# Two sequences per loop body: query, key and feed-forward projections for both at once, 256 columns wide, as three split float32r products

## What is computed

```python
def _L1_xattn_ref(x, mem_out, ...):
    xn = rms_norm(x, attn_norm_w)
    q, k, v = jnp.split(xn @ to_qkv_w, 3, axis=-1)        # 128 -> 3 * 1024
    q, k, v = (split_heads(q), split_heads(k), split_heads(v))
    q, k = (rope(q), rope(k))
    kf = jnp.concatenate([k_extra, pm, k], axis=2)
    ...
    probs = jax.nn.softmax(scores, axis=-1)
    o = jnp.einsum('bhij,bhjd->bhid', probs, vf)
    x = x + o.transpose(0, 2, 1, 3).reshape(b, n, HEADS * DH) @ to_out_w
    h = rms_norm(x, ff_norm_w) @ ff_w1 + ff_b1             # 128 -> 2 * 341
    a, g = jnp.split(h, 2, axis=-1)
    return x + jax.nn.silu(g) * a @ ff_w2 + ff_b2
```

## Time and profile before

| | |
|---|---|
| median of 3 runs | 1442.05 us (1441.9 to 1442.86) |
| the profiled execution, its own time | 1442.24 us |
| its span, first to last instruction | 1440.5 us |
| mean granted TensorE clock over the span | 0.991 |
| period of a steady turn (one sequence) | 21.21 us |
| DMA queues' share of the 16 engines' time | 27.8% |

### The profile page before, as it was taken

The page is one execution under the profiler, slowest core; times in us unless marked ns, Lnnn a source line. Parts: engine busy times, 40 slices in busy tenths (PEclk is TensorE's granted clock), DMA queues, the critical chain, the costliest instruction groups (busy, mean ns, idle before and its releaser), DMA issues.

```text
span 1440.5 us, 54339 instructions
## 1 busy us (share of the span) xinstructions
PE 1388.4 (96%) x20771; PEld 1225.9 (85%) x20771; DVE 1045.2 (73%) x3025; ACT 790.7 (55%) x1933; POOL 817.6 (57%) x1169
## 2 busy tenths in 40 slices
PE   2699999999999999999999999999999999999997
PEld 1578888988888888898898888889889888888986
DVE  4457777777777777777777777777777777777763
ACT  1245565565556556556556555655655655565553
POOL 1246556556556655655655665565565566566553
PEclk9989999999999999999999999999999999999998
DMA  6323222222322222222232222222222223222210
GB/s 187 113 69 102 101 71 100 101 80 92 103 92 86 100 101 71 100 101 76 96 103 91 87 100 97 75 100 101 74 98 101 87 89 103 93 81 100 101 45 26
DMA packets 106146, 133.13 MB, mean 92 GB/s; under 512 B 16310, under 2 KB 88523, under 8 KB 105995
## 3 DMA queue, kind: packets, MB, share of 16 engines
q1 hardware_dynamic: 106122, 132.81, 27.8%
HBM read 41.04 MB, written 24.61 MB: 46 GB/s over the span
## 4 chain that ended last, share of the span: by engine, by line
PE 94%; DMA 2%; DVE 2%; ACT 1%; SPq 1%; issue 1%; POOL 0%; POOLq 0%; ACTq 0%; DVEq 0%
PE psum L926 16%; PE psum L962 11%; PE psum L975 10%; PE psum L1005 8%; PE psum L989 6%; PE psum L968 5%; PE psum L939 5%; PE psum L982 4%; PE psum L1119 4%; PE psum L933 4%; PE psum L953 2%; PE psum L1041 2%; PE psum L919 2%; PE psum L920 2%; PE psum L921 2%; PE psum L1018 2%
## 5 line engine op out<-in xcount | busy, mean ns | idle before, releaser
L620 ACT ACTIVATE probs<-psum 81x512 f32<-81x512 f32 x256 | 151.0, 591 | 285.0 <-PE psum L968 285.0
L926 PE MATMUL psum<-xnT,wqkv 128*128 128x128 f32 x2048 | 268.3, 280 | 0.0
L736 DVE TENSOR_TENSOR ra<-psum,rope 128x512 f32<-128x512 f32 x256 | 175.0, 684 | 112.1 <-PE psum L926 112.1
L926 PEld LDWEIGHTS psum<-xnT,wqkv 128*128 128x128 f32 x2048 | 248.0, 195 | 0.2 <-ACT xnT L568 0.2
L537 POOL TENSOR_TENSOR ug<-tanh_gate,half_gate 128x384 f32<-128x384 f32 x64 | 64.2, 1003 | 281.7 <-ACT half_gate L611 281.7
L500 POOL TENSOR_SCALAR z<-z 77x512 f32<-77x512 f32 x256 | 156.6, 621 | 101.2 <-DVE z L741 101.2
L741 DVE TENSOR_TENSOR z<-psum,wT 77x512 f32<-77x512 f32 x256 | 163.5, 679 | 39.2 <-PE psum L933 39.2
L962 PE MATMUL psum<-qT,kall 64*81 64x64 f32 x4096 | 177.1, 237 | 0.0
L745 DVE TENSOR_REDUCE mx<-psum 128x4 f32<-128x324 f32 x256 | 119.6, 488 | 77.7 <-PE psum L953 77.7
L962 PEld LDWEIGHTS psum<-qT,kall 64*81 64x81 f32 x4096 | 159.5, 149 | 18.0 <-issue 12.5
L736 DVE TENSOR_TENSOR rb<-psum,rope 128x512 f32<-128x512 f32 x256 | 174.2, 681 | 0.0
(11 more groups left out here) (137 smaller groups left out, 2588.2 us busy)
## 6 DMA issues: line engine op xcount, KB each, us to landing
rs<-rb SPq DMA_DIRECT2D x256, 256.0 KB, 2.4
qk_dram<-qk_parts SPq DMA_DIRECT2D x64, 307.5 KB, 4.1
qk_stack<-qk_dram SPq DMA_DIRECT2D x256, 76.9 KB
seq_in<-in SPq DMA_DIRECT2D x64, 166.5 KB
out<-out_sb SPq DMA_DIRECT2D x64, 64.0 KB, 1.6
maskT<-in SPq DMA_DIRECT2D x64, 38.5 KB
vall<-memv_dram SPq DMA_DIRECT2D x128, 4.0 KB, 1.9
ctx_all<-in SPq DMA_DIRECT2D x5, 320.0 KB, 5.7
```

What stands on the lines that cost most here:

```text
L620: return nc.scalar.activation(probs[:, 4 * t:4 * t + 4, :].rearrange("k n i -> k (n i)"), at(f"score{t}")[0:KEYS, :], ACT.Exp, scale=float ...
L736: last = V.tensor_tensor(dst[:, place(name)].rearrange("p (c i) -> p c i", c=4), p, rope[:, n, :].unsqueeze(1).broadcast_to([128, 4, S]), ...
L926: last = mm(at(name)[:, S * n:S * (n + 1)], wqkv[:, lo + 128 * n:lo + 128 * (n + 1)], xnT[:])
```

## The change

The body of every engine's loop now does two sequences: turns run over n = -6, -4, ... 62, and a piece is named for a sequence of the pair, ".0" or ".1". What is done for both at once has no suffix: "xnT", "q0" to "q3" and "k0" to "k3", "hnT", "gate", "lin" and "both" (the third, 85-row, block of gate and linear part together). `project_turned` now takes two 128x128 blocks of the weights for one name, each as three float32r products over 256 moving columns (128 of each sequence), and so does `into_ff`. Weights are split once at the start (`wqkv_hi`, `wqkv_lo`, `w1_hi`, `w1_lo`); `hnT` is split in each turn as `xnT` is. `ra`, `rb`, `rs`, `qT` and `kall` hold both sequences. The tables and the weights that the start needs share memory with them. All orders and the banks in `tasks` are others.

The core of the diff (of the new table one stretch only; the bodies of the engines are given by their orders below it):

```diff
-LEAD = 4
-QK = ("q0", "k0", "q1", "k1")
+LEAD = 6
+QK = ("q0", "k0", "q1", "k1", "q2", "k2", "q3", "k3")
 
...
-        wqkv = sb("wqkv", [D, 3 * INNER])
-        wv_hi, wv_lo = (sb(n, [D, INNER], F32R) for n in ("wv_hi", "wv_lo"))
+        wqkv_hi, wqkv_lo = (sb(n, [D, 3 * INNER], F32R) for n in ("wqkv_hi", "wqkv_lo"))
         wout = sb("wout", [128, PAIRS, D])
         wmem = sb("wmem", [D, D])
-        w1 = sb("w1", [D, 2 * DFF])
+        w1_hi, w1_lo = (sb(n, [D, 2 * DFF], F32R) for n in ("w1_hi", "w1_lo"))
...
-        ra = sb("ra", [S, 2 * INNER])
-        rb = sb("rb", [S, 2 * INNER])
-        rs = sb("rs", [S, 2 * INNER])
-        qT = sb("qT", [128, PAIRS, S])
-        kall = sb("kall", [128, PAIRS, NSEG, KEYS])
+        y_keep = sb("y_keep", [S, 2, D])
+        xnT = sb("xnT", [D, 2, S])
+        xnT_hi, xnT_lo = sb("xnT_hi", [D, 2, S], F32R), sb("xnT_lo", [D, 2, S], F32R)
+        rot = sb("rot", [128, 2 * 4 * INNER])
+        ra, rb = rot[:, 0:4 * INNER], rot[:, 4 * INNER:]
+        rs = sb("rs", [128, 4 * INNER])
+        qT = sb("qT", [128, PAIRS, 2, S])
+        kall = sb("kall", [128, PAIRS * 2 * NSEG, KEYS])
...
-                turn = ahead + (place - back) // len(users)
+                turn = ahead + 2 * ((place - back) // len(users))
...
-                done = {k: n + k for k in range(0, LEAD + 2)}
+                seq = {lead: live(n, lead) for lead in range(0, LEAD + 2)}
+                done = {k: n + k for k in range(-1, LEAD + 3)}
                 body(n, seq, done)
 
-            for n in range(-LEAD, 1):
+            for n in range(-LEAD, 1, 2):
                 turn(n)
-            with eng.Fori(1, B - LEAD) as n:
+            with eng.Fori(2, B - LEAD - 1, 2) as n:
                 turn(n)
-            for n in range(B - LEAD, B + 0):
+            for n in range(B - LEAD, B, 2):
...
+            ("pv2.1", 1, 3, (o2_ready,)),
+            ("q3", 2, 5, (q3_rotated,)),
+            ("k2", 5, 5, (k2_rotated,)),
+            ("q2", 0, 5, (q2_rotated,)),
+            ("v1.0", 3, 4, (v1_kept,)),
...
+                if seq[3] is not None:
+                    sp.wait_ge(q3_rotated, done[4])
...
+                if seq[5] is not None:
+                    sp.wait_ge(k1_rotated, done[6])
+                    passed(sp, sp_passed)
+                    for odd in range(2):
+                        sp.dma_start(rs[odd::2, 2 * BANK:4 * BANK], rb[1 - odd::2, 2 * BANK:4 * BANK]).then_inc(swapped1_in, 16)
+                    sp.wait_ge(q0_rotated, done[6])
+                    passed(sp, sp_passed)
+                    for odd in range(2):
+                        sp.dma_start(rs[odd::2, 0 * BANK:2 * BANK], rb[1 - odd::2, 0 * BANK:2 * BANK]).then_inc(swapped0_in, 16)
...
-                    pool.wait_ge(z1_masked, done[4])
+                    pool.wait_ge(swapped0_in, done[4] * 16)
+                    summed("k0")
+                    summed("q0").then_inc(q0_summed, 2)
+                    pool.wait_ge(swapped3_in, done[4] * 16)
+                    summed("q3")
+                    summed("k3")
+                    pool.wait_ge(swapped2_in, done[4] * 16)
+                    summed("q2")
+                    summed("k2").then_inc(k2_summed, 2)
...
+                if seq[1] is not None:
+                    pool.wait_ge(hnT_hi_ready, done[2])
+                    nc.gpsimd.tensor_tensor(hnT_lo[:], hnT[:], hnT_hi[:].bitcast(F32), ALU.subtract).then_inc(hnT_lo_ready, 2)
...
+                    pool.wait_ge(xnT_hi_ready, done[6])
+                    nc.gpsimd.tensor_tensor(xnT_lo[:], xnT[:], xnT_hi[:].bitcast(F32), ALU.subtract).then_inc(xnT_lo_ready, 2)
+                    if first(seq[4]):
+                        pool.wait_ge(w_hi_ready, 1)
+                        nc.gpsimd.tensor_tensor(wqkv_lo[:], wqkv, wqkv_hi[:].bitcast(F32), ALU.subtract).then_inc(w_lo_ready, 1)
+                        pool.wait_ge(w_hi_ready, 2)
+                        nc.gpsimd.tensor_tensor(w1_lo[:], w1, w1_hi[:].bitcast(F32), ALU.subtract).then_inc(w_lo_ready, 1)
...
+            def product(dst, columns, w_hi, w_lo, hi, lo):
+                mm(dst, w_hi[:, columns], hi, stop=False)
+                mm(dst, w_hi[:, columns], lo, start=False, stop=False)
+                return mm(dst, w_lo[:, columns], hi, start=False)
...
             def project_turned(name):
-                lo = INNER * "qk".index(name[0]) + BANK * int(name[1])
-                for n in range(4):
-                    last = mm(at(name)[:, S * n:S * (n + 1)], wqkv[:, lo + 128 * n:lo + 128 * (n + 1)], xnT[:])
+                for n in range(2):
+                    lo = INNER * "qk".index(name[0]) + 128 * (2 * int(name[1]) + n)
+                    last = product(at(name)[:, 2 * S * n:2 * S * (n + 1)], slice(lo, lo + 128), wqkv_hi, wqkv_lo, xT_hi, xT_lo)
                 return last
 
...
-            def into_ff(name, part):
-                for n in range(FCH):
-                    lo = DFF * part + 128 * n
-                    last = mm(at(name)[0:FROWS[n], S * n:S * (n + 1)], w1[:, lo:lo + FROWS[n]], hnT[:])
-                return last
+            def into_ff(dst, part, n):
+                lo = DFF * part + 128 * n
+                return product(dst, slice(lo, lo + FROWS[n]), w1_hi, w1_lo, hT_hi, hT_lo)
 
...
+                        pe.wait_ge(w_lo_ready, 2)
+                    free(pe, "k0", n, 5)
+                    pe.wait_ge(xnT_lo_ready, done[6])
+                    project_turned("k0").then_inc(k0_filled, 2)
+                    free(pe, "k3", n, 5)
+                    project_turned("k3").then_inc(k3_filled, 2)
+                    free(pe, "q1", n, 5)
+                    project_turned("q1").then_inc(q1_filled, 2)
...
+                if seq[5] is not None:
+                    free(pe, "q3", n, 5)
+                    project_turned("q3").then_inc(q3_filled, 2)
+                    free(pe, "k2", n, 5)
+                    project_turned("k2").then_inc(k2_filled, 2)
+                    free(pe, "q2", n, 5)
+                    project_turned("q2").then_inc(q2_filled, 2)
                 if seq[4] is not None:
```

More of the change, by code:

```diff
@@ L444, in body @@
+                if seq[6] is not None:
+                    sp.wait_ge(parts_out, done[7] * 16)
                     passed(sp, sp_passed)
@@ new lines, in body @@
+                if seq[1] is not None:
+                    free(pe, "hnT", n, 1)
+                    pe.wait_ge(hn_ready, done[2])
+                    for c in range(2):
+                        last = nc.tensor.transpose(at("hnT")[:, S * c:S * (c + 1)], hn[:, c, :], ident[:])
+                    last.then_inc(hnT_filled, 2)
+                if seq[2] is not None:
+                    free(pe, "shift.0", n, 2)
+                    pe.wait_ge(mt_ready, done[3])
+                    mm(at("shift.0")[0:2 * H, 0:S], mt[:].rearrange("i p h -> i (p h)"), ident_b[:]).then_inc(shift_filled, 1)
+                    free(pe, "score2.0", n, 2)
+                    free(pe, "score3.0", n, 2)
+                    scores(0, 1)
@@ new lines, in body @@
+                if seq[6] is not None:
+                    free(pe, "pv.0", n, 6)
+                    pe.wait_ge(u_kept, done[7])
+                    for g in range(GROUP):
+                        last = nc.tensor.transpose(at("pv.0")[:, S * g:S * (g + 1)], u[:, S * g:S * (g + 1)], ident[:])
+                    last.then_inc(pv_filled, 1)
+                if seq[3] is not None:
+                    pe.wait_ge(shift_ready, done[4])
+                    less_maxima(1, 2).then_inc(score2_filled, 1)
@@ new lines, in body @@
+                if seq[0] is not None:
+                    free(pe, "down.0", n, 0)
+                    pe.wait_ge(sT2_ready, done[2])
+                    for i in range(FCH):
+                        last = mm(at("down.0")[:, 0:D], sT[0:FROWS[i], i, 0, :], w2[0:FROWS[i], i, :], start=i == 0, stop=i == FCH - 1)
+                    last.then_inc(down_filled, 1)
+                if seq[5] is not None:
+                    free(pe, "q0", n, 5)
+                    project_turned("q0")
+                    free(pe, "k1", n, 5)
+                    project_turned("k1").then_inc(k1_filled, 2)
@@ new lines, in body @@
+                if seq[1] is not None:
+                    free(pe, "down.1", n, 1)
+                    for i in range(FCH):
+                        last = mm(at("down.1")[:, 0:D], sT[0:FROWS[i], i, 1, :], w2[0:FROWS[i], i, :], start=i == 0, stop=i == FCH - 1)
+                    last.then_inc(down_filled, 1)
+                if seq[7] is not None:
+                    free(pe, "xs0.1", n, 7)
+                    free(pe, "xs1.1", n, 7)
+                    cross_scores(1, 0, 1).then_inc(xs01_filled, 1)
```

1269 lines of the change are left out of this document (792 added, 477 removed).

## The result

The changed kernel takes 1464.42 us (median of 4, 1460.65 to 1471.4), the kernel before 1442.03 (median of 4 beside it): a ratio of 1.016, interval 1.014 to 1.018. It is 1.6% slower, where 1378 us and 4.4% faster were forecast. The profiled execution took 1460.65 us, its span is 1458.8.

A forecast was written before the change was run, and what follows sets the result against it. PE's sequence was taken to bound the kernel: 39.75 us work plus 0.4 waits per pair, 32 x 40.15 = 1284.8, plus 91.1 for start and end, 1375.9 us of span, hence 1378 us; forecast range 1352 to 1412 (0.68).

The forecast's parts named there:

- I take 0.4 us: Steady turn: PE's waits at handoffs per pair of sequences, taken as 0.4 us, bounds 0 and 1.5.
- The handoffs named: Rotary stretch and maxima: PE waits none at qkv.0, about even at oT1.1, 0.3 us at max2.0.
- DVE's list is that of before but for the gating: VectorE, steady turn: same instructions except three gating ones for six; at most 32.2 of the 39.75 us.
- A pair needs 39.75 us of PE: PE's steady work per pair without waits: 42.42 - 10.06 - 0.30 + 7.69 = 39.75 us.
- 8 us more: First and last turns: 83.1 us outside the steady periods grow by 8 to 91.1; bounds 0 and 20.
- near 74: Start: first projection k0 begins near 74 us, about 16 us later than 57.92.
- I expect most of that to be won back: Start: most of k0's 16 us delay returns, as the second sequence's projections and self attention follow in the same turn.
- some 5 us: Start, ahead of k0: the second sequence's cross attention adds some 5 us.
- rival (3): Projection passes on PE: a pass costs over 0.147 us, so the kernel ends slower; chance 0.05 for a dearer pass.
- exposed loads: Projection passes on PE: weight load adds to each pass, 0.30 us per pass, total time 1763 us; chance 0.01.
- 10.06 us removed: PE, per pair: the plain float32 instructions of L926 and L989 go, 2 x 5.03 = 10.06 us.
- Rival (1): From k0 to max2.0: handoffs cost more, waits of 1.5 to 2.3 us a pair, 1413 to 1440 us; chance 0.14.

The follow-up runs named there:

- e1: Changed kernel with VectorE's hn.0 and t0g moved behind the two maxima max0.0 and max1.0: 1430.37 us, 0.9907 of the kernel before.
- e6: Kernel before plus one spare VectorE SBUF-to-SBUF product per sequence, placed amid GpSimd's sums: 1538.4 us, 1.0652 of the kernel before.
- e11: Kernel before plus the same spare VectorE product per sequence, placed behind hn, away from GpSimd's sums: 1444.35 us, 1.000 of the kernel before.
- e5: e1 with GpSimd's weight split moved ahead of xnT_lo but behind VectorE's casts of the tables: 1423.15 us, 0.9862 of the kernel before.
- e10: e5 with ScalarE's xnT_hi put ahead of its copies for the memory tokens in the first turns: 1420.35 us, 0.9842 of the kernel before.
- e3: Changed kernel with GpSimd splitting the weights ahead of xnT_lo in place of behind it: 1463.1 us.
- e9: e5 with one plain float32 product in place of the three float32r passes, still 256 columns: 1469.12 us, 1.0171 of the kernel before.
- e7: e1 with each 256-column pass of the split projections written as two of 128 columns: 1629.6 us, measured once.

## Why the prediction was wrong

**Waits, "I take 0.4 us", upper bound 1.5.** The handoffs named (qkv.0, oT1.1, max2.0) show no wait in a steady turn of the changed kernel, and the run of sums, forecast from 10.5 to 20.7 us behind k0, stands there from 10.7 to 20.7. In e1 PE is idle for 0.3 us of a period. But 0.93 of the 1.03 us that PE is idle in the changed kernel's period stand at max0.0, by a mechanism that no sentence of the prediction has. The failed step is "DVE's list is that of before but for the gating": the list was, the company was not. In the order of after, hn.0 and t0g stand beside GpSimd's run of sums; in that of before both stand behind it, t0g beside a clamp (0.39 us) and hn with GpSimd idle at its start (0.28). I had both orders and the place of GpSimd's run, and did not lay one over the other. The Trainium skill ("SBUF — State Buffer", Who interferes with whom) has the rule: VectorE and GpSimd share a pair of SBUF ports, held exclusively, and a tensor_scalar in a fast mode or an instruction with two SBUF inputs asks for it. The traces agree in which instructions wait (L981, t0g, xn) and which don't (those with an operand in PSUM, and L1165 and L978); which mode an instruction runs in, no trace here shows. They add that the wait mostly reached over several instructions of GpSimd. Price: 41.93 - 40.95 = 0.98 us a period, 31 us in all; e1 gives back 31 in the span, e6 and e11 show the cause alone.

**"A pair needs 39.75 us of PE".** It needs 40.72 (e1), 31 us more in all. The pass was 0.119 where 0.1165 was taken. Three of the six first passes cost 0.17 to 0.32, which the sum has not. All 66 together take 8.3 us (from the end of each one's predecessor to its own end) where 7.69 were forecast. This is the size of a term, within its bound of 8.4; why these first passes are dearer was not tried. The remaining 0.4 us I did not trace to the end; part of it is that the transposes of hn, which were to save 0.15 us, add 0.41 for the two and a gap of 0.1 ahead of them.

**Start and end, "8 us more", bound 20.** It was 34 more. Two steps failed: k0 "near 74" came 14.6 us later than that, and "I expect most of that to be won back" took 8 us off the 16 where the ends grew by 3.3 more than k0's delay; 14.6 and 11.3 are the 25.9 us. Nothing is won back. Against before:

| kernel | k0 at, later by | ends (span - 32 periods), more by |
|---|---|---|
| before | 57.92 | 83.1 |
| after | 88.55, 30.6 | 117.0, 33.9 |
| e1 | 89.86, 31.9 | 117.7, 34.6 |
| e5 | 84.03, 26.1 | 111.7, 28.6 |
| e10 | 82.67, 24.8 | 108.4, 25.3 |

The split's 8.2 us were priced right (8.6), but the terms named, 8.6 and "some 5 us", add up to 13.6 and not to 16, and the 5 was too small: without the split in the path (e10) k0 is still 24.8 us late. The chain above shows what stands there: one more load of inputs (4.67 us) and one more trip through DRAM (3.96 and 2.35), of the third sequence, which the prediction does not have in the path.

By its own rows the clock is the smaller part of the ends. The mean granted clock over the span is 0.991 in before, 0.984 in the changed kernel, 0.987 in e1 and 0.988 in e10. My estimate from these: what the clock can have cost is at most its shortfall times the span, 13, 23, 19 and 17 us. Set against before that is 10 of the changed kernel's 34 us more, 6 of e1's 35 and 4 of e10's 25, as far as the column shows it; no run separates the clock from the rest. The clock can also account for e3's profiled run (0.979, 31 us by the same estimate), which is 6 us longer than the changed kernel's with k0 only 0.5 later. The idle time before k0 alone does not decide it: in e10 PE works 9.2 of the ten microseconds from 80 us, and the clock still falls to 0.73 and 0.76 in the windows from 100 to 120 us.

**What held.** The price of a pass: 0.119 us, against rival (3) with over 0.147 and against the 0.30 of exposed loads; no engine becomes the bound by its sum; 10.06 us removed. The slower result had a chance of 0.09, for a dearer pass or for waits beyond 2.5 us, and neither happened; no rival has the ends. Rival (1) had the right place, "one chain of DVE and POOL", and a wrong mechanism, and with 1440 us as its end it did not reach the time either. The 83 us that the span is over the forecast are 31 us of this wait, 31 of PE work, 26 of the ends, less 5 of waits that I had in the sum and that e1 does not show.

The change has one good part and two bad ones: split arithmetic at 256 columns wins 46 us (e9 against e5), while the paired turns lose 34 at the ends (25 in e10) and, in this order, 31 to the wait for GpSimd. Repaired (e10), it is 1.6% faster than before.

## What to carry to other kernels

When an order moves, lay over GpSimd's runs those of VectorE's instructions that were held here: a tensor_scalar over 128 x 128 from SBUF to SBUF (hn, xn, the spare one) and what reads two operands in SBUF (t0g). Price each that falls into a run with the rest of that run; put what TensorE waits for ahead of it. An instruction whose duration jumps beside the same shape elsewhere is waiting, even if its engine counts as busy. What delays the first piece of a pipeline's steady work was paid in full here (the table), so keep once-only work off the chain that leads to it, and away from VectorE instructions that it would hold.

## What the runs showed of the hardware

- A VectorE instruction held by GpSimd mostly waits for the end of a run of back-to-back sums, not of the one under way: in 29 of 31 turns (after) and 60 of 62 (e6), up to 3.66 us beside sums of 1.26 (after), 3.59 in e6. In the others, and in e3, it got in behind the instruction under way.
- Not every VectorE instruction within SBUF is held: BATCH_NORM_STATS2 over 128 x 128 took 0.28 us and a tensor_scalar over 128 x 1 0.15 us amid the same run (after).
- A float32r pass over 128 columns with 128 x 128 weights costs 0.111 us, over 256 columns 0.119 (e7, e1): the second half of the width is nearly free. Three such passes of 256 columns cost 0.36 us against 0.43 for the two plain float32 ones (0.216 each from start to start, e9); at 128 columns it is 0.33 against 0.23 (0.114 each). So the split gains over float32 only when wide.
